# Self attentions of a four-block transformer chain: queries and keys in f32 on four groups of 32 rows instead of stacks of bf16 parts, products issued in pairs

## The reference

```python
# L2: rope on q and k, a mask of blocks; L3: biases on q, k, v, no mask
s = jnp.einsum('bqhd,bkhd->bhqk', q, k) * scale
s = jnp.where(mask, s, jnp.finfo(s.dtype).min)
a = jax.nn.softmax(s, axis=-1)
return jnp.einsum('bhqk,bkhd->bqhd', a, v)
```

## Time and profile before

| | us |
|---|---|
| median of 3 runs | 2857.09 (2856.45 to 2859.88) |
| the profiled execution's own time | 2857.61 |
| its span, first to last instruction | 2856.3 |
| TensorE busy | 2416.1 (85%) |
| VectorE busy | 1738.5 (61%) |
| ScalarE busy | 1280.9 (45%) |
| GpSimd busy | 338.4 (12%) |

### The profile page before, as it was taken

The page is one execution under the profiler, slowest core; times in us unless marked ns, Lnnn a source line. Parts: engine busy times, 40 slices in busy tenths (PEclk is TensorE's granted clock), DMA queues, the critical chain, the costliest instruction groups (busy, mean ns, idle before and its releaser), DMA issues.

```text
span 2856.3 us, 37239 instructions
## 1 busy us (share of the span) xinstructions
PE 2416.1 (85%) x13127; PEld 1239.0 (43%) x13127; DVE 1738.5 (61%) x5398; ACT 1280.9 (45%) x2434; POOL 338.4 (12%) x350
## 2 busy tenths in 40 slices
PE   6778678878987979999888899988889988899668
PEld 2456334544554444454344445442234332234335
DVE  5545856575334565557866665657676677775343
ACT  2324434443222214455435555545656646656434
POOL 3101333243020100000200000000000010000201
PEclk8889788889998888999999999998999999999879
DMA  4556231000001130000422100043120032110110
GB/s 153 166 127 190 89 101 59 17 25 8 1 8 30 56 73 12 12 23 12 135 77 57 42 16 12 17 128 92 45 45 12 23 110 80 42 27 12 54 50 15
DMA packets 150926, 160.65 MB, mean 56 GB/s; under 512 B 33391, under 2 KB 120258, under 8 KB 150476
## 3 DMA queue, kind: packets, MB, share of 16 engines
q1 hardware_dynamic: 150740, 158.28, 19.1%
HBM read 97.39 MB, written 60.19 MB: 55 GB/s over the span
## 4 chain that ended last, share of the span: by engine, by line
PE 64%; DVE 18%; ACT 6%; DMA 4%; issue 4%; POOL 2%; SPq 2%; ACTq 0%; POOLq 0%; DVEq 0%
PE bank L1145 9%; PE bank L1646 8%; PE bank L1117 7%; PE bank L1092 7%; PE bank L1667 5%; PE bank L2120 4%; PE bank L1121 3%; PE bank L756 3%; PE bank L1568 3%; DVE max L1218 3%; PE bank L2297 2%; DVE bank L1215 2%; PE bank L2122 2%; PE bank L683 2%; ACT work L1159 1%
## 5 line engine op out<-in xcount | busy, mean ns | idle before, releaser
L1159 ACT ACTIVATE work<-bank 128x512 f32<-128x512 f32 (+1 forms) x1216 | 702.4, 597 | 586.1 <-PE bank L1121 263.2
L1215 DVE CUSTOM_DVE_ANT_0 bank<-bank,weights 128x512 f32<-128x512 f32 x512 | 349.5, 702 | 195.4 <-PE bank L1092 193.8
L1218 DVE TENSOR_REDUCE max<-bank 128x1 f32<-128x512 f32 x512 | 340.9, 685 | 138.2 <-PE bank L1092 136.4
L1092 PE MATMUL bank<-k_stack,q_stack 97*128 97x512 bf16 x896 | 361.4, 406 | 69.0 <-DVE max L1215 28.6
L1117 PE MATMUL bank<-q_stack,k_stack 99*128 99x512 bf16 x896 | 346.7, 389 | 12.5 <-ACT work L1159 9.7
L1646 PE MATMUL bank<-hT,weights 128*128 128x512 f32 x512 | 265.5, 621 | 13.0 <-ACT work L1692 6.3
L1121 PEld LDWEIGHTS bank<-ident_b,weights 128*128 128x128 bf16 x2048 | 159.7, 98 | 119.2 <-issue 10.3
L1092 PEld LDWEIGHTS bank<-k_stack,q_stack 97*128 97x128 bf16 x896 | 89.7, 100 | 271.6 <-DVE max L1215 102.5
L1121 PE MATMUL bank<-ident_b,weights 128*128 128x128 bf16 x2048 | 200.5, 220 | 0.0
L1667 PE MATMUL bank<-weights,work 128*128 128x256 f32 x768 | 196.4, 384 | 0.0
L1667 PEld LDWEIGHTS bank<-weights,work 128*128 128x128 f32 x768 | 140.9, 190 | 60.3 <-issue 40.9
(11 more groups left out here) (242 smaller groups left out, 3652.3 us busy)
## 6 DMA issues: line engine op xcount, KB each, us to landing
q_stack<-parts_q SPq DMA_DIRECT2D x60, 384.0 KB, 3.8
parts_q<-parts SPq DMA_DIRECT2D x46, 384.0 KB, 2.6
k_stack<-parts_k SPq DMA_DIRECT2D x40, 384.0 KB, 4.8
weights<-parts_q SPq DMA_DIRECT2D x36, 384.0 KB, 4.0
parts_q<-parts SPq DMA_DIRECT2D x46, 256.0 KB, 2.9
parts_k<-parts SPq DMA_DIRECT2D x24, 384.0 KB, 2.5
parts_k<-parts SPq DMA_DIRECT2D x24, 256.0 KB, 2.9
weights<-in_L_e_w SPq DMA_DIRECT2D x12, 512.0 KB, 5.5
```

The lines of the kernel that those rows point to most:

```text
L1092: m = pe.e.matmul(bank.ap[:, :], self.q(g)[0:MAX_ROW, h, qt * P:(qt + 1) * P], k_stacks[self.key, g].ap[0:MAX_ROW, h, half * BLK:(half + 1 ...
L1159: ac.e.activation(p.ap[0:self.nk, :], banks[self.key, "exp", g, i].ap[0:self.nk, :], ACT.Exp).then_inc(*probs.tick((self.key, g, i)))
L1215: ve.e.tensor_tensor_reduce(bank[:, :], bank[:, :], mask_bias[:, qt, half * BLK:(half + 1) * BLK], 1.0, -3.4e38, ALU.add, ALU.max, to).the ...
L1218: ve.e.tensor_reduce(to, bank[:, :], AX_X, ALU.max).then_inc(*maxima.tick((self.key, g, i)))
```

## The change

- `Heads` takes the place of `Parts` for k and q of both self attentions. Each head gets 32 rows of its own, 16 of them used. An item is 4 heads by 512 tokens: eight f32 matmuls of 16 columns (four column groups by two halves of the channels). There are 8 items for each tensor, where `Parts` had 4. ScalarE writes f32 with scale and bias by row, rope is as before, and one DMA stores the tile. Nothing is split in parts.
- `SelfAttention` takes the place of `Attention` of kind full. Four heads ("quad", two groups) are loaded at once as f32, 128 rows by 1024; two quads fit at a time. A tile of scores is one f32 matmul of 16 rows (17 with the maximum for the exponentials), on the row group of its head. Groups alternate between the lower and the upper two row groups.
- On every second beat the waits for two max tiles and two exp tiles come first, then the four matmuls, then L2's masks. Maxima travel as f32.
- L2 and L3 both have period 38 and lags (32, 38, 43, 71). The constant rows and the third stack go, with their memsets; `QueryRows` puts ones into stacks for a later cross attention.

```diff
-        full_of = dict(max_banks=(0, 1), exp_banks=(2, 3), pv_banks=(4,), lags=(32, 40, 46, 74))
+        full_of = dict(period=38, lags=(32, 38, 43, 71))
...
+        class Heads(Stage):
...
+                    for i in range(CC):
+                        for j in range(QUAD):
+                            at = self.col + (QUAD * q + j) * D
+                            m = pe.e.matmul(bank.ap[j * ROW:j * ROW + D, :], w[:, i, at:at + D], hT[self.b][:, bl, i, :],
+                                            start=i == 0, stop=i == CC - 1, tile_position=(0, j * ROW))
+                    m.then_inc(*dense.tick(k))
...
+        class SelfAttention(Attending):
...
+            max_banks, exp_banks, pv_banks, nprob = (0, 1), (2, 3), (4,), 7
...
+            def tile(self, g, h):
+                return ((g % 2 * PAIR + h) * ROW, 0)
...
+            def tensor(self, pe):
+                turns = 0
+                for beat in range(self.beats):
+                    tops, exps = self.group(beat, 0, self.n), self.group(beat, self.exp_at, self.n)
+                    if tops and tops[1] % 2 == 0:
+                        for h in range(PAIR):
+                            self.ready_top(pe, tops[0], tops[1] + h, turns + h)
+                        turns += PAIR
+                    if exps and exps[1] % 2 == 0:
+                        for h in range(PAIR):
+                            self.ready_exp(pe, exps[0], exps[1] + h)
+                    if tops and tops[1] % 2 == 0:
+                        for h in range(PAIR):
+                            self.top_tile(pe, tops[0], tops[1] + h)
+                    if exps and exps[1] % 2 == 0:
+                        for h in range(PAIR):
+                            self.exp_tile(pe, exps[0], exps[1] + h)
+                        if self.mask:
+                            for h in range(PAIR):
+                                self.mask_tile(pe, exps[0], exps[1] + h)
...
+            def ready_top(self, pe, g, i, turn):
+                bank = banks.take(self.max_banks[turn % 2], (self.key, "max", g, i), (maxima, (self.key, g, i)))
+                for f in bank.free:
+                    pe.wait_ge(*f)
...
-            st["k3"] = Parts(lane_d, b, "L3", "k", st["n7"], "L3qkv", C, 1.0, column("L3_b_qkv", CC), None, drams)
+            st["k3"] = Heads(lane_d, b, "L3", "k", st["n7"], "L3qkv", C, lambda q: 4 + q, st["self2"].last_loads(ld_k))
...
-            st["self3"] = Attention(lane_a, b, "L3", "full", st["q3"], st["k3"], (V, V_late)[b], [(vec, (st["v3"].key, "all"))],
-                                    [(dense, (st["v3"].key, "all"))], rows_ready=k_rows + [("third", 0)], keys_ready=[],
-                                    period=32, stacks=(0, 1, 2), stacks_free=[(pool_done, ("third", 0))], **full_of)
+            st["self3"] = SelfAttention(lane_a, b, "L3", st["q3"], st["k3"], (V, V_late)[b], [(vec, (st["v3"].key, "all"))],
+                                        [(dense, (st["v3"].key, "all"))], stacks_free=topk_left, **full_of)
```

More of the change, by code:

```diff
@@ L34 @@
 PAIR = 2
+QUAD = 4
+ROW = 32
 GROUPS = H // PAIR
@@ L309, in build_program @@
                    for b in range(B)]
+        heads_dram = [{n: nc.dram_tensor(f"heads_{n}{b}", [QUAD * P, S], F32, kind="Internal").ap() for n in "qk"}
+                      for b in range(B)]
         kx_dram = [nc.dram_tensor(f"parts_kx{b}", [C, PRODUCTS, LC], BF16, kind="Internal").ap() for b in range(B)]
@@ L322, in build_program @@
         ld_tm = [count(f"ld_tm{b}", 16) for b in range(B)]
+        st_heads = [count(f"st_heads{i}", 16) for i in range(4)]
+        ld_heads = count("ld_head_cols", 16)
         st_parts = [count(f"st_parts{i}", 16) for i in range(4)]
@@ L997, in __init__ @@
                 self.own = kind != "context"
-                self.n = PAIR * NT * NB if kind == "full" else PAIR * NB
+                self.n = PAIR * NB
                 self.in_a = 0 if lane is lane_a else 1
@@ L1116, in exp_tile @@
                 else:
-                    m = pe.e.matmul(bank.ap[0:self.nk, :], self.k(g, h, STACK, kt * P), q, start=True, stop=not self.mask)
-                    if self.mask:
-                        pe.wait_ge(*vec["mask"])
-                        for j in range(TPB):
-                            m = pe.e.matmul(bank.ap[:, j * P:(j + 1) * P], mask_bias[:, half * TPB + j, kt * P:(kt + 1) * P],
-                                            ident_b[:, :], start=False, stop=j == TPB - 1)
+                    m = pe.e.matmul(bank.ap[0:self.nk, :], self.k(g, h, STACK, kt * P), q, start=True, stop=True)
                 m.then_inc(*exp_scores.tick((self.key, g, i)))
@@ L1180, in vector @@
                         self.max_of(ve, *now)
-                    if now := self.group(beat, self.rows_at, 1):
-                        if self.kind == "full":
-                            g = now[0]
-                            m1 = max1.take(g % 2 + 2 * self.in_a, (self.key, g), (turned, (self.key, "rows", g)))
-                            for f in m1.free:
-                                ve.wait_ge(*f)
-                            ve.wait_ge(*maxima[self.key, g, self.n - 1])
-                            ve.e.tensor_reduce(m1.ap[:, :], max2[self.key, g].ap[:, :, :], AX_X, ALU.max).then_inc(
-                                *maxima.tick((self.key, g, "rows")))
                     yield
@@ L1193, in max_of @@
                 if i == 0:
-                    if self.kind == "full":
-                        m2 = max2.take(g % 2, (self.key, g), (maxima, (self.key, g, "rows")))
-                        for f in m2.free:
-                            ve.wait_ge(*f)
-                    else:
-                        m1 = max1.take(g % 2 + 2 * self.in_a, (self.key, g), (turned, (self.key, "rows", g)))
+                    m1 = max1.take(g % 2 + 2 * self.in_a, (self.key, g), (turned, (self.key, "rows", g)))
@@ new lines, in max_of @@
+                    for f in m1.free:
+                        ve.wait_ge(*f)
+                ve.wait_ge(*max_scores[self.key, g, i])
+                ve.e.tensor_reduce(max1[self.key, g].ap[:, i * TPB:(i + 1) * TPB],
+                                   banks[self.key, "max", g, i].ap[:, 0:TPB * self.nk].rearrange("p (i n) -> p i n", n=self.nk), AX_X,
+                                   ALU.max).then_inc(*maxima.tick((self.key, g, i)))
+                if i == self.n - 1:
+                    maxima.also((self.key, g, "rows"), (self.key, g, i))
@@ L1200, in max_of @@
                         for f in m1.free:
                             ve.wait_ge(*f)
+                        ve.wait_ge(*maxima[self.key, g, self.n - 1])
+                        ve.e.tensor_reduce(m1.ap[:, :], max2[self.key, g].ap[:, :, :], AX_X, ALU.max).then_inc(
+                            *maxima.tick((self.key, g, "rows")))
+                    yield
+            def max_of(self, ve, g, i):
+                if i == 0:
+                    m2 = max2.take(g % 2, (self.key, g), (maxima, (self.key, g, "rows")))
+                    for f in m2.free:
+                        ve.wait_ge(*f)
+                h, qt, half = i % PAIR, i // PAIR // NB, i // PAIR % NB
+                to = max2[self.key, g].ap[:, h * NT + qt, half:half + 1]
@@ L1202, in max_of @@
                 bank = banks[self.key, "max", g, i].ap
                 ve.wait_ge(*max_scores[self.key, g, i])
-                if self.kind != "full":
-                    ve.e.tensor_reduce(max1[self.key, g].ap[:, i * TPB:(i + 1) * TPB],
-                                       bank[:, 0:TPB * self.nk].rearrange("p (i n) -> p i n", n=self.nk), AX_X, ALU.max).then_inc(
-                        *maxima.tick((self.key, g, i)))
-                    if i == self.n - 1:
-                        maxima.also((self.key, g, "rows"), (self.key, g, i))
-                    return
```

324 lines of the change are left out of this document (263 added, 61 removed).

## The result

| | us | ratio to before (95% interval) |
|---|---|---|
| before, 4 runs beside | 2858.49 (2856.45 to 2864.45) | |
| changed, 4 runs | 3551.93 (3531.28 to 3560.63) | 1.2411 (1.2353 to 1.247) |
| changed, profiled execution | 3531.28, span 3529.9 | |

A forecast was written before the change was run, and what follows sets the result against it. TensorE, busy 85% of the span, was taken to bound the kernel, with 213 us idle in S1 to S4. Terms 55 + 90 + 55 + 9 + 22 - 13 = +218 on 2857.6 gave 3076 us, range 2920 to 3289.

The forecast's parts named there:

- Term 1: Score tiles in S1 to S4: four f32 products on row groups stream together, 0.862 us a set; +55 us.
- partial overlap: Rival: row groups overlap only in part, first weight loads going one after another; +328 us, about 3400, half 3240; chance 0.09.
- of none: Rival: row groups do not overlap at all, 3.45 us a set; +1420 us, about 4500; chance 0.03.
- Term 2: Changes of the array's division in S1 to S4: 844 more at 0.107 us each, +90 us.
- Term 3: `Heads` replacing `Parts`: 8 items instead of 4 for each of 8 tensors, 1.72 us each; +55 us.
- the memsets: Memsets that go: four ahead of S1, 7.2 us, and three ahead of S3, 5.4; together -13 us.
- Term 4: Sets waiting for both max and exp banks: 2.55 us round trip, 222 us short, set against 213 idle; +9 us net.
- Term 5: Group changes in L3: the next set waits for the rows of travelling maxima, short in S3 and S4; +22 us.
- What was promised of S4: S4, the lightest stretch, should grow most in proportion, its 84 sets with too little behind them leaving TensorE waiting.

The follow-up runs named there:

- e12: The kernel before with score products reading 64 of their 97 and 99 rows, the other parts and the maximum's subtraction left out: 3094 us, ratio 1.084.
- e5: The kernel before with bf16 score products in sets of four behind common waits, and paired maxima and exponentials side by side: 3067 us, ratio 1.075.
- e1: The changed kernel with each score product reading all 32 rows of its row group, the added rows zeros: 3316 us, ratio 1.161.
- e7: e1 with L3's attentions back at period 32 and lags (32, 40, 45, 73): 3382 us, ratio 1.185.
- e8: The kernel before with score products reading 16 rows instead of 97 and 99, lower parts and the maximum's subtraction left out: 3469 us, 2 runs.
- e9: The kernel before with 32 columns of `v` in `pv` instead of 17, the added sums not read: 2861 us, ratio 1.001.
- e11: e1 with 32 columns for the products with the values: 3315 us, ratio 1.161.
- e10: e9 with exp products over all 128 rows instead of 99: 2862 us, ratio 1.002.
- e2: The kernel before with two max and two exp tiles as one set behind common waits every second beat, VectorE and ScalarE order kept: 3201 us, ratio 1.121.

## Why the prediction was right or wrong

**Term 1, the score tiles: right.** The timeline shows a pair of sets in S4 at full clock:

```profile
3000.19 0.70 PE L1417 MATMUL bank<-k_stack,q_stack 16*128 16x512 f32 x2
3000.20 0.70 PE L1424 MATMUL bank<-q_stack,k_stack 17*128 17x512 f32 x2
...
3000.72 0.59 PE L1417 MATMUL bank<-k_stack,q_stack 16*128 16x512 f32 x2
...
3001.35 1.29 DVE L1511 TENSOR_REDUCE max<-bank 128x1 f32<-128x512 f32 x2 [3.61 <-PE bank L1417]
3001.49 1.09 ACT L1465 ACTIVATE work<-bank 128x512 f32<-128x512 f32 x2 [3.81 <-PE bank L1424]
...
3002.74 0.70 PE L1417 MATMUL bank<-k_stack,q_stack 16*128 16x512 f32 x2 [1.41 <-DVE max L1511]
```

Four f32 products stream side by side. From a set to the next matmul it is 1.07 us in the undisturbed cases, in the promised 0.95 to 1.1, against 3.45 in a row: 3.2 times. The Trainium skill (page "TensorE: Matmul & The Clock Gate", section on Part 3, packing small matmuls) has 3.07 for four row tiles, which makes 1.12 us (an estimate, 3.45 / 3.07); the trace is a little better. The rivals of partial overlap and of none fall.

**Term 2, changes of division: right at full clock.** `pv`'s 0.107 for a change was carried over to row groups without a row to show it. A set is 1.07 - 0.86 = 0.21 over one stream, two changes, 0.105 each, and e12 shows 0.09 to 0.10 with products that stand alone. Counted in the traces there are 1374 changes in S1 to S4 instead of 600, so 774 more where 844 were taken. Terms 1 and 2 with the items of term 3 in S1 to S4 made 186, the walk finds 205.

**Term 3, Heads: right.** An item of L915 takes 1.84 us in the chain above, within 1.7 to 2.0, and S1 starts 12 us later where 14 for the items less 7 for the memsets were expected.

**Term 4, the wait for a pair: the round trip right, its sum wrong.** The second set above starts 2.55 us after the first, as worked out. The maxima start 1.16 after the set. The waits of the changed kernel:

```profile
PEld bank L1417 <- DVE max L1511: 222.8, 147, 3.2
...
PEld bank L1417 <- DVE max L1508: 149.6, 127, 3.6
PE bank L1417 <- DVE max L1511: 86.3, 102, 2.3
```

Idle time ahead of max tiles is 186 us by the walk, 222 were forecast. The step that failed is the next one: "Set against the 213 us idle before, which the same waits made, this is +9." Only 93 of the idle time before lay ahead of a max tile; the rest, 157 us, lay ahead of other instructions and stayed, 177 now. By the same prices the term should have been 222 - 93 = +129, not +9. The stretches had been read as a total of idle time, and the waits as its only cause; the trace of before would have told the difference. Two runs bear it out. In e5 pairs alone add 170 us of idle time and 214 in all, in a kernel with no row groups and no added passes; in e1, with most of the clock given back, idle time is 428 us, 178 over before.

**Term 5, group changes: too high.** In S3 and S4 the next set hardly waits for the rows of maxima; this is the only such wait listed:

```profile
PE bank L1417 <- DMA q_stack<-max_parts: 0.5, 2, 0.3
```

At the 16 ends of groups TensorE is idle for some 32 us in all, but nearly all of it ahead of other instructions than the set. The work of the beats between covered the travel, in e1 too (0.2 us), so the 22 us didn't come. That idle time ahead of everything but max tiles grew by 20 us is no proof of the term. And keeping 32 beats was no better in e7 (+65), with its 48 doubled sets.

**What no term held: the clock, +339.** This is the step that took the time out of the range. Every duration came from rows at full clock, and the sum put the clock at nothing without a word on it; before it had been 0.93 to 0.97 in these stretches, and now it is 0.86 to 0.70. The Trainium skill (same page, section on Part 1, the clock gate) has the clock depend on how busy TensorE has lately been. The profile's busy time can't test that here, for a slow product counts as busy for longer. What can be compared are kernels with the same instructions and waits that differ in the rows read: changed and e1 (16 or 17 rows against 32), e8 and e12 (16 against 64). In both pairs the kernel with more rows had the higher clock in every stretch:

| score products read | kernel | clock in S1 to S4 |
|---|---|---|
| 97 and 99 rows, fewer changes of division | before | .95 .97 .93 .97 |
| 64 rows | e12 | .94 .93 .82 .87 |
| 16 rows | e8 | .64 .70 .69 .64 |
| 4 x 32 rows | e1 | .92 .96 .88 .91 |
| 4 x 16 or 17 rows | changed | .86 .86 .74 .70 |

S3 and S4, where the score products are the largest part of TensorE's work, suffer most. Why the rows matter to the clock, no run shows; and what is left between e1 and before (.92 .96 .88 .91 against .95 .97 .93 .97) may be the changes of division, the waits or the rows of single products. The lower clock also lengthens the round trip of term 4, since the maxima wait for the slower set:

```profile
2990.88 1.22 PE L1417 MATMUL bank<-k_stack,q_stack 16*128 16x512 f32 x2
...
2991.89 1.06 PE L1417 MATMUL bank<-k_stack,q_stack 16*128 16x512 f32 x2
...
2992.99 1.29 DVE L1511 TENSOR_REDUCE max<-bank 128x1 f32<-128x512 f32 x2 [3.02 <-PE bank L1417]
...
2994.38 1.22 PE L1417 MATMUL bank<-k_stack,q_stack 16*128 16x512 f32 x2 [0.61 <-DVE max L1511]
```

The maxima start 2.11 us after the set instead of 1.16, and the next set after 3.50 instead of 2.55. All of that growth is the slower set itself, though, and slower work elsewhere fills waits: e1 has more idle time than the changed kernel, not less. So the terms can't be added cleanly.

Taken together for S1 to S4: forecast 186 + 9 + 22 and 5 off for the memsets, 212; found 205 + 113 + 339, 657. With the clock held at its old share the kernel would have come to 3552 - 339, about 3210, if nothing else moved, and to some 3270 if idle time grows on as it did in e1 (there 214 us came back of 279): estimates both, and both inside the range, though 130 to 190 over the forecast, most of which is term 4. So two steps failed, the clock put at nothing and the 213 us set against the new wait. What was promised of S4 came true in part for another reason: at 559 us instead of 355 it did grow most in proportion, at the lowest clock of the four.

## What to carry to other kernels

Count idle time by what stands behind it before setting a new wait against an old one: only the idle time ahead of the same instruction can be taken over. Packing small products in row groups streams them side by side, but with f32 it only bought back the passes here, and filling the rows with zeros was worth 236 us; look at the granted clock of the stretch before trusting any duration of TensorE. When a product is made smaller in a trial, look whether the time to its neighbours still is what it was. And where an engine in order waits for several buffers together, work out the whole round trip and compare it with the work between two such waits.

## What the runs showed of the hardware

- TensorE's granted clock was higher where its products read more rows: the same kernel went from 0.70 to 0.91 in S4 when 16 rows became 32, though the added ones hold zeros, and e8 and e12 from 0.64 to 0.87 with 64 rows instead of 16. Between 97 and 64 rows (0.97 and 0.87) the changes of division grew as well. Columns (17 to 32, in e9 and e11) and 128 rows instead of 99 (e10) made no difference that could be measured. Whether rows do it alone or together with passes and idle time wasn't measured by itself; the kernels with idle TensorE and full rows (e2, e5) also lost some.
- At the lower level a set took 2.02 us and at the upper 1.07, an item of L999 1.81 and 0.92.
- Four f32 products of 16 or 17 rows and 512 columns, each on its row group, took 1.07 us together; four on only two row groups took 1.92 (e7).
- A change between the full array, row groups and column groups cost 0.09 to 0.11 us at full clock. Products of 64 and of 16 rows paid it too without being told a place in the array (0.31 us to the mask instead of 0.22, in e12 and e8).
